# Attention with an FP4 feed-forward on one core: the next pair's score maxima are transposed later, fewer score tiles run ahead, and the denominators are inverted and divided later

## The reference

```python
qkv = xn @ W_attn + b_attn                    # 16 heads of 32
att = softmax(where(causal, q @ k.T * 32**-0.5, -inf))
y   = (att @ v) @ W_proj + b_proj
h   = silu(fp4(xn) @ fp4(w_gate).T) * (fp4(xn) @ fp4(w_up).T)
out = x + y + fp4(h) @ fp4(w_down).T          # fp4: blocks of 16, quantised and back
```

## Time and profile before

| | us |
|---|---|
| median of 3 runs | 3881.24 (3878.92 to 3884.07) |
| the profiled execution | 3882.22 |
| its span, first to last instruction | 3880.4 |

### The profile page before, as it was taken

The page is one execution under the profiler, slowest core; times in us unless marked ns, Lnnn a source line. Parts: engine busy times, 40 slices in busy tenths (PEclk is TensorE's granted clock), DMA queues, the critical chain, the costliest instruction groups (busy, mean ns, idle before and its releaser), DMA issues.

```text
span 3880.4 us, 63776 instructions
## 1 busy us (share of the span) xinstructions
PE 3755.6 (97%) x21836; PEld 2704.8 (70%) x21836; DVE 2627.6 (68%) x3834; ACT 1217.0 (31%) x2313; POOL 933.6 (24%) x462
## 2 busy tenths in 40 slices
PE   8999999999999999999999889999999999999999
PEld 6556557557556556556565548888888888888887
DVE  6665665666766756765665547777777777777777
ACT  2441541532532532523523422222222222222222
POOL 0550550650641631632622530000000000000000
PEclk9999999999999999998998899999999999999999
DMA  6425426335335335335245440111110111111111
GB/s 198 98 78 180 98 77 184 82 97 164 79 113 154 87 105 160 75 122 150 70 152 156 115 163 27 32 32 32 32 32 32 32 32 32 32 32 32 32 32 32
DMA packets 178222, 337.02 MB, mean 87 GB/s; under 512 B 42432, under 2 KB 50112, under 8 KB 176832
## 3 DMA queue, kind: packets, MB, share of 16 engines
q1 hardware_dynamic: 153504, 275.75, 25.0%
q10 hardware_dynamic: 24480, 58.21, 4.4%
HBM read 213.92 MB, written 118.43 MB: 86 GB/s over the span
## 4 chain that ended last, share of the span: by engine, by line
PE 89%; DVE 4%; issue 3%; DMA 2%; SPq 1%; POOL 1%; ACT 1%; ACTq 0%; DVEq 0%; POOLq 0%
PE f_ps L1492 25%; PE ps_dense L984 13%; PE f_ps_o L1504 12%; PE ps_st L1036 8%; PE ps_s L1009 7%; PE ps_dense L1149 4%; PE ps_y L1055 4%; PE ps_dense L1055 3%; PE ps_dense L1073 3%; PE ps_dense L1009 2%; PE ps_st L1043 1%; PE f_ps L1484 1%; DMA den<-rob 1%; DVE mx L629 1%; PE ps_s L1014 1%
## 5 line engine op out<-in xcount | busy, mean ns | idle before, releaser
L1492 PE MATMUL f_ps<-wgu,xqt 128*128 128x512 f32 (+1 forms) x4608 | 992.6, 373 | 1.4 <-DVE xqt L1352 1.4
L1492 PEld LDWEIGHTS f_ps<-wgu,xqt 128*128 128x128 f32 x4608 | 842.2, 188 | 122.8 <-DVE xqt L1352 1.7
L908 ACT ACTIVATE pt<-ps_st 128x512 f32<-128x512 f32 (+3 forms) x1152 | 568.6, 526 | 649.7 <-PE ps_st L1036 378.0
L629 DVE TENSOR_REDUCE mx<-ps_s 128x1 f32<-128x640 f32 (+3 forms) x576 | 553.4, 961 | 295.6 <-PE ps_s L1014 294.4
L561 POOL TENSOR_TENSOR stage<-stage,pt 128x1536 f32<-128x1536 f32 (+2 forms) x176 | 519.2, 2950 | 46.8 <-ACT pt L908 35.1
L1504 PE MATMUL f_ps_o<-wd,hqt 128*128 128x512 f32 x2112 | 510.9, 394 | 0.6 <-DVE hqt L1378 0.6
L559 POOL TENSOR_TENSOR stage<-pt 128x1792 f32<-128x1792 f32 x64 | 256.8, 4013 | 988.0 <-ACT pt L908 988.0
L1504 PEld LDWEIGHTS f_ps_o<-wd,hqt 128*128 128x128 f32 x2112 | 390.8, 188 | 79.0 <-DVE hqt L1378 0.8
L984 PE MATMUL ps_dense<-arena,wa 128*128 128x512 f32 x1536 | 390.2, 401 | 11.6 <-DVE rob L677 6.1
L984 PEld LDWEIGHTS ps_dense<-arena,wa 128*128 128x128 f32 x1536 | 280.0, 190 | 72.6 <-issue 10.7
L1036 PE MATMUL ps_st<-stack 98*128 98x512 f32 (+3 forms) x768 | 271.3, 416 | 0.0
(11 more groups left out here) (130 smaller groups left out, 4980.8 us busy)
## 6 DMA issues: line engine op xcount, KB each, us to landing
qk_scratch<-stage SPq DMA_DIRECT2D x128, 512.0 KB, 2.9
stack<-qk_scratch SPq DMA_DIRECT2D x192, 256.0 KB
arena<-qk_scratch SPq DMA_DIRECT2D x192, 256.0 KB
xs<-in_L_attn_x SPq DMA_DIRECT2D x64, 256.0 KB, 3.7
rob<-in_L_attn_x ACTq DMA_DIRECT2D x64, 256.0 KB, 2.8
acc_scratch<-rob ACTq DMA_DIRECT2D x64, 256.0 KB, 2.2
xt<-in_L_attn_x SPq DMA_DIRECT2D x64, 256.0 KB, 2.6
at<-acc_scratch SPq DMA_DIRECT2D x64, 256.0 KB, 2.6
```

Source lines behind the costliest of these rows:

```text
L629: nc.vector.tensor_reduce(mx[:, h * ST + q:h * ST + q + 1], scores_bank(p, n)[:, 0:(q + 1) * P], axis=AX.X, op=ALU.max, negate=True).then_ ...
L908: nc.scalar.activation(exps(kt)[:, h, q - kt * P:q - kt * P + n], ps_st[:, w % ST_RING, 0:n], ACT.Exp, scale=SCALE).then_inc(st_exp, 1)
L1492: last = nc.tensor.matmul(ps[:, SLOT[c], gu, 0:n].rearrange("p (j n) -> p j n", n=P), xqt[:, a, k], wgu[:, b, gu * FC + f // P:gu * FC + ( ...
```

## The change

- `STEPS` is rewritten. MAX moves from the end of unit 1 to the middle of unit 4. `EARLY` becomes 3, so pair p computes tiles 3 to 15 of pair p+1 before MAX and tiles 0 to 2 of pair p+2 behind it. P3 joins P5, P6 and P7 among the products done in the next pair. Before, the eight units held 4, 3, 3, 3, 0, 2, 0, 1 tiles; now they hold 4, 3, 4, 2, 1, 1, 1, 0.
- `VECTOR_STEPS`: INV moves from behind the seventh row maximum of the pair to behind the eleventh, MAX from there to behind the thirteenth. The division is that of p-2 and not of p-1, in two halves (Y0, Y1) around the fourth row maximum.
- On SP the store of the inverses is split from their broadcast and goes ahead of the next pair's maxima.
- At the start of a batch the three early tiles of pair 1 lie beside V6 and V7 (`BESIDE`), pair 0's own tiles move two places earlier, and `maxima(0)` goes into the middle of V6. The early tiles use `ps_s` alone, each waiting for the one before it. The wait for the whole of v moves to the first product with v. The loads of pair 1's stack start one projection earlier.
- The wait for `m_in` moves behind the T that lie ahead of S0.

```diff
-    STEPS = ["T MT S0 S1 T MT S2 T S3 MT M2 P5 T M3 MT DEN P6",
-             "S0 S1 S2 T MT T MT M2 S3 T MT M3 P7 P0 MAX",
-             "S0 T S1 S2 T MT M2 P1 T MT S3 M3",
-             "S0 T MT S1 S2 T MT M2 S3 T M3",
-             "S0 M0 MT S1",
-             "S0 T S1 T M1- MT M0 M1 P2 P3",
-             "S0 S1",
-             "S0 T MT M0- M1- M0 P4 S1 M1"]
-    VECTOR_STEPS = "R R R R DEN R R R MAX INV R R R R R R R Y R R"
+    STEPS = ["T T MT P3 P5 T MT S0 S1 T S2 S3 M2 MT M3 P6 DEN P7",
+             "S0 S1 S2 T MT T MT M2 T S3 MT M3",
+             "S0 S1 T S2 T MT M2 P0 S3 T T MT M3 P1",
+             "S0 T T MT S1 S2 S3 M2 P2",
+             "S0 M3- M0 MAX T S1 MT M1",
+             "S0 T S1 M0 MT M1",
+             "S0 T MT M0 P4 S1",
+             "S0 S1 M1- M0 M1"]
+    VECTOR_STEPS = "R R R Y0 R Y1 DEN R R R R R R R INV R R MAX R R R"
...
-        return ps_s[:, :] if p == 0 or n % 2 == 0 else ps_dense[:, 0]
+        return ps_s[:, :] if p == 0 or (p == 1 and n < EARLY) or n % 2 == 0 else ps_dense[:, 0]
...
+    BESIDE = {half: (0, n) for n, half in enumerate(HALVES[-EARLY - 2 - TILES:-EARLY - 2])}
+    BESIDE[HALVES[-EARLY - 1]] = "MAX"
+    BESIDE.update({half: (1, n) for n, half in enumerate(HALVES[-EARLY:])})
...
                 if p:
                     den_rows(p - 1)
+                    inverses(p - 1)
                 if p + 1 < PAIRS:
                     maxima(p + 1)
                 if p:
                     spread(p - 1)
...
-                    elif p and p < PAIRS - 1:
-                        divide(p - 1)
+                    elif p > 1:
+                        divide(p - 2, [int(step[1])])
...
-            pe.wait_ge(v_done, ONE + b * ST + ST)
-            for n in range(EARLY):
-                scores(1, n)
-                mask_scores(1, n)
             due, unmasked = 0, []
             for p in range(PAIRS):
-                pe.wait_ge(m_in, ONE + b * PAIRS * 2 * DMA + (p + 1) * 2 * DMA)
```

More of the change, by code:

```diff
@@ L251, in attention @@
     LOADS = 7
-    LOADS_AFTER = {GROUP0 - 1: LOADS, **{i: 1 for i in range(9, NQK)}}
+    LOADS_AFTER = {GROUP0 - 1: LOADS, **{i: 1 for i in range(8, NQK - 1)}}
     def w_stage(k):
@@ L352, in x_bank @@
         return ps_st[:, t % ST_RING]
-    HALVES = [(use, half) for use in PROJ for half in (0, 1)][-3 - TILES:-3]
-    FIRST = {half: n for n, half in enumerate(HALVES)}
+    HALVES = [(use, half) for use in PROJ for half in (0, 1)]
+    BESIDE = {half: (0, n) for n, half in enumerate(HALVES[-EARLY - 2 - TILES:-EARLY - 2])}
+    BESIDE[HALVES[-EARLY - 1]] = "MAX"
+    BESIDE.update({half: (1, n) for n, half in enumerate(HALVES[-EARLY:])})
     NEEDS = {("QK", i): (c + 1) * PER for i, (_, _, c) in enumerate(QK)}
@@ L479, in den_rows, with inverses, spread @@
                                  dn[r * HD:r * HD + 1].rearrange("o (a k) -> o a k", k=den.shape[1])).then_inc(den_in, DMA)
-            def spread(p):
+            def inverses(p):
                 sp.wait_ge(inverted, ONE + b * NDEN + p + 1)
                 sp.dma_start(inv_scratch.rearrange("h (a k) -> (h a) k", k=den.shape[1]), inv[:, :]).then_inc(inv_out, DMA)
+            def spread(p):
                 sp.wait_ge(inv_out, ONE + b * NDEN * DMA + (p + 1) * DMA)
@@ L655, in invert_last, with divide @@
                 nc.vector.reciprocal(dn, den_bank(PAIRS - 1)).then_inc(last_inverted, 1)
-            def divide(p):
+            def divide(p, halves=(0, 1)):
                 dve.wait_ge(pv_done, ONE + b * PAIRS * ST + (p + 1) * ST)
@@ L663, in divide @@
                 first = p % 2 * HP
-                for s in range(2):
+                for s in halves:
                     rows = slice(s * HP, (s + 1) * HP)
@@ L737, in body @@
                 kind, i = use
[L738 to L741, removed]
+                if BESIDE.get((use, 0)) == "MAX":
+                    split_max(0)
+                elif (use, 0) in BESIDE:
+                    row_max(*BESIDE[use, 0])
+                if (use, 1) in BESIDE and kind == "QK":
+                    row_max(*BESIDE[use, 1])
                 {"T": lambda t: low_of_x(b, t), "QK": low_of_qk, "V": v_of}[kind](i)
+                if (use, 1) in BESIDE and kind == "V":
+                    row_max(*BESIDE[use, 1])
                 for step, *args in aside.get(use, []):
@@ L763, in body @@
                         low_of_unit(2)
-                if use == PROJ[-2]:
-                    split_max(0)
-            for n in range(EARLY):
-                row_max(1, n)
             due = 0
@@ L980, in split_product @@
                 for n, (k, lh, rh) in enumerate(terms):
-                    if n == len(terms) // 2 and (use, 0) in FIRST:
-                        scores(0, FIRST[use, 0])
-                        mask_scores(0, FIRST[use, 0])
+                    if n == len(terms) // 2 and BESIDE.get((use, 0)) == "MAX":
+                        maxima(0)
+                    elif n == len(terms) // 2 and (use, 0) in BESIDE:
+                        scores(*BESIDE[use, 0])
+                        mask_scores(*BESIDE[use, 0])
                     last = nc.tensor.matmul(bank(*use), left(lh, k), right(rh, k), start=n == 0, stop=n == len(terms) - 1)
                 last.then_inc(d_full, 1)
-                if (use, 1) in FIRST:
-                    scores(0, FIRST[use, 1])
-                    mask_scores(0, FIRST[use, 1])
+                if (use, 1) in BESIDE:
+                    scores(*BESIDE[use, 1])
+                    mask_scores(*BESIDE[use, 1])
             def scores(p, n):
@@ L997, in scores @@
                                + (p // SLOTS + 1) * LOADS * DMA)
+                if p == 1 and n == EARLY + (EARLY + 1) % 2:
+                    pe.wait_ge(v_done, ONE + b * ST + ST - 1)
                 if (n == 0 and p == 1) or (n == 1 and p > 1):
@@ L1002, in scores @@
                     pe.wait_ge(den_copy, ONE + b * NDEN + p - 1)
-                pe.wait_ge(s_max, ONE + b * PAIRS * TILES + p * TILES + max(n - 1, 0) if p else
-                           ONE + b * PAIRS * TILES + n)
+                alone = p == 0 or (p == 1 and n < EARLY)
+                pe.wait_ge(s_max, ONE + b * PAIRS * TILES + p * TILES + (n if alone else max(n - 1, 0)))
                 qs = stack(p)[0:KS, h, q * P:(q + 1) * P]
@@ L1032, in transposed_scores @@
                 w = p * NPARTS + PART0[kt] + i
+                if (kt, i) == (0, 0):
+                    pe.wait_ge(m_in, ONE + b * PAIRS * 2 * DMA + (p + 1) * 2 * DMA)
                 pe.wait_ge(st_exp, ONE + b * PAIRS * NPARTS + max(w - ST_RING + 1, 0))
@@ L1046, in times_v @@
             def times_v(p, kt):
-                if kt == 0 and p > 1:
+                if kt == 0 and p == 0:
+                    pe.wait_ge(v_done, ONE + b * ST + ST)
+                elif kt == 0 and p > 1:
                     pe.wait_ge(y_div, ONE + b * PAIRS * 2 + (p - 1) * 2)
```

3 lines of the change are left out of this document (removed).

## The result

The changed kernel takes 3783.1 us (3781.9 to 3786.8), the kernel before in the same comparison 3880.2 us (3878.9 to 3884.1): ratio 0.975, 95% interval 0.9733 to 0.9767. That is 97 us saved, where 122 were forecast; 3783 lies in the forecast's range, above the likeliest case's own (3740 to 3780). The profiled execution took 3783.6 us with a span of 3781.8. First the changed kernel's page, its first line and the line of busy time.

The account below looks back on a forecast made before the run. The prediction took PE, busy for 97% of the span, to bound the kernel. Its terms, 8 x (6.0 + 2.7 + 3.3 + 0.8) + 20 = 122 us, off 3882 and less 1 us to the median, gave 3759 us, range 3708 to 3808.

Parts of the forecast that it names:

- the likeliest case: Whole kernel: the forecast 3759 us, with its own range 3740 to 3780; chance 0.48.
- (a): Start of a batch: V7's end to S0 falls from 10.1 to 3.3 us; gain 6.0 us a batch.
- (b): Pair 0: the low clock goes in every second batch; gain 2.7 us a batch, between 0 and 5.4.
- The rival in which it never falls: Pair 0: two short waits do not lower the clock, 5.4 us gained in all batches; 3737 us, chance 0.20.
- (c): Pairs 1 to 5: DVE's inversion wait goes, cycle 19.3 us; gain 3.3 us a batch, between 0 and 5.3.
- POOL was not late next: Steady pairs: POOL's sums were named the next limit, so a cycle cannot be under 18.9 us.
- (d): Pair 6: six more tiles, some 2.3 us, fill PE's wait for POOL; gain nothing.
- (e): Pair 7: the clock holds once idle time is gone; gain 0.8 us a batch, between -0.5 and 1.5.
- (f): Last batch's long cycles: inversion waits shrink to 1.5 to 3 us in three; gain 20 us, between 5 and 29.
- The broadcast has landed about 1 us before Y0: Steady pairs: the inverses' broadcast lands about 1 us before the division's first half, so no new wait there.
- The range's ends: 3708 us: no clock fall, best steady pairs and last batch; 3808 us: falls everywhere, worst start of a batch.
- clumps of tiles: Each cycle: T T tiles wait for DVE and the clock falls, 7.1 us x 40 cycles; 4089 us, chance 0.06.

## Why the prediction was right, and where not

**(a) Start of a batch:** right in mechanism, 6.7 us a batch against 6.0: 3.3 us from V7 to S0 as forecast, with two waits of 0.99 and 0.59 against 1.2 and 0.8, and V6 and V7 longer by 0.4 together instead of 0.8. The kernel before lost 10.1 to 10.9 us there, 10.4 on the mean, and the sum took batch 2 with 10.1.

**(b) The clock:** "every second batch" came out as five of eight. It was a guess between two rows. The runs fit that the waits make it: with 0.33 and 0.33 us no batch falls, with four waits of 0.6 to 1.15 all do, and between these it goes either way. Why it goes one way in one batch and the other in the next stays open. The rival in which it never falls was wrong for this kernel. The advice on idle gaps in the Trainium skill (TensorE: Matmul & The Clock Gate, "Why this matters for your kernels") would let waits this short pass; these runs don't.

**(c) Steady pairs:** the term that was mis-sized, 13.6 us instead of 23. Two steps failed, in opposite directions. The forecast counted 0.6 us a cycle for PE's weight loads standing idle; most of that time ran beside matmuls, and taking the inversion's wait away gave 0.1 us on the mean. And it said that the work is the same; the new order made the same matmuls 0.3 us shorter, partly by fewer switches and, as far as the traces tell, partly by fewer tiles that wait for a row maximum, and no term held that. The window of one cycle, PE 19.88 of 19.88 us, would have warned that the inversion's wait was worth little. POOL was not late next; PE was.

**(d), (e) Pairs 6 and 7:** as forecast; the wait for POOL covered the six tiles, and the low clock behind it is gone in all batches (19.1 us to the output projection, where six of eight had 19.6 to 21.5).

**(f) The last batch:** 9.9 us instead of 23.3, the largest miss. The inversion's wait was handled rightly (1.5 to 3 us in three cycles; it was 7.0 us in three). "The broadcast has landed about 1 us before Y0" was a step of term (c) only: it was not asked again for the batch in which these transfers take nearly three times as long. Taken up there, 7.45 us of broadcast against that 1 us of margin, it would have given waits of this size. And where the forecast had one low clock, these waits made three, about half of the loss.

The range's ends, added up as the forecast says, come out at 3712 and 3815 and not at 3708 and 3808; 3783 lies well inside either. Of the rivals, clumps of tiles cost nothing here; but the run with fewer switches shows that the kernel stands close to that edge.

## What to carry to other kernels

Before pricing a wait on the engine that bounds the kernel, look at one whole cycle of that engine: if it has no gap there, idle weight loads and waits of others are worth little (0.1 us a cycle here), and what is left is its own work, whose price can hang on the order of the same instructions. Little is not nothing: where ends are modelled, waits of 0.2 us hide in busy time, and only the starts show them, by an instruction that starts just behind its releaser and a neighbour ahead of it that took longer than its form takes elsewhere. A transfer that is moved needs its margin checked in the stage with the most traffic, not in the steady one. Two repairs of the same cost are run together before they are added: here the second turned the first into a late transfer.

## What the runs showed of the hardware

- A float32 score matmul behind a bf16 mask costs 0.07 us more than behind its like (four such places: 0.28 us a cycle, at full clock, with no gap on PE). In one cycle of the changed kernel, where nothing waits, a score matmul of 512 columns keeps its place for 226 to 249 ns, up to the start of the next score matmul, if another score matmul stood ahead of it, for 312 to 323 ns if a mask did, and for 332 to 335 ns if a float32 product with v did, so the type alone is not the reason.
- Small transfers beside megabytes of loads slowed: the fold from 2.71 us to 6.3 and 7.2, and there a part of the broadcast took 7.45 and the store of the inverses 6.6 us.
- PE's busy time hid waits: with masks moved later the cycle grew by 0.61 us, of which PE's idle time shows 0.33.
- The clock did not answer the same work in the same way: with one order in pair 0 and the same wait of 0.85 us the granted clock fell in three of eight batches of one kernel and in none of another.
